# A fifth late expert: its weights loaded and split within the block loop, the experts in natural order, three turns written out

## What is computed

```python
x = _layernorm(x + attention(x, w_qkv, w_out))
probs = softmax(x @ gate_w.T)                     # 16 experts
_, idx = top_k(probs + gate_b, 6)                 # cw: probs of the chosen, else 0
for W1, B1, W2, B2, W3, B3, c in experts:         # 16 of them, H = 176
    h = silu(x @ W1.T + B1) * (x @ W3.T + B3)
    y = y + c[:, None] * (h @ W2.T + B2)
z = silu(x @ ws1.T + bs1) * (x @ ws3.T + bs3) @ ws2.T + bs2     # HS = 352
x = _layernorm(x + y + z)
```

## Time and profile before

| what | us |
| --- | --- |
| median of 3 runs | 1139.32 |
| the runs | 1139.49, 1139.32, 1127.47 |
| the profiled execution, its time | 1130.5 |
| its span, first to last instruction | 1128.7 |

### The profile page before, as it was taken

How to read it: one execution, slowest core, us unless ns; L and a number is a source line. 1 busy time by engine, 2 the same in 40 slices (tenths; PEclk the granted TensorE clock), 3 DMA queues, 4 the chain that set the end, 5 groups by cost and what they waited for, 6 DMA issues and landing times.

```text
span 1128.7 us, 28318 instructions
## 1 busy us (share of the span) xinstructions
PE 1036.1 (92%) x8028; PEld 847.3 (75%) x8029; DVE 748.7 (66%) x2401; ACT 670.9 (59%) x1680; POOL 740.6 (66%) x676
## 2 busy tenths in 40 slices
PE   7899998989898998788998999999999999999991
PEld 4546464646464644387988999999999999999991
DVE  8786878786878787577765555555555555555455
ACT  3567676767676765665555555555555555555544
POOL 4224368787878888877635666666666666666665
PEclk9999999999999998899998999999999999999996
DMA  6624254545454535557867666677776666667593
GB/s 185 183 71 114 77 143 147 164 147 163 148 161 145 169 124 172 189 174 228 287 165 139 115 120 119 114 118 117 119 118 113 110 116 113 116 116 140 82 313 144
DMA packets 127037, 163.54 MB, mean 145 GB/s; under 512 B 18800, under 2 KB 107504, under 8 KB 126704
## 3 DMA queue, kind: packets, MB, share of 16 engines
q1 hardware_dynamic: 82240, 99.73, 31.6%
q0 software_dynamic: 39024, 54.29, 25.6%
q10 hardware_dynamic: 5696, 8.55, 2.4%
HBM read 65.36 MB, written 73.85 MB: 123 GB/s over the span
## 4 chain that ended last, share of the span: by engine, by line
PE 63%; DMA 12%; DVE 12%; issue 5%; ACT 4%; POOL 2%; SPq 1%; ACTq 0%; POOLq 0%; DVEq 0%
PE psum L1057 13%; PE psum L794 10%; PE psum L1084 10%; DMA z_d<-y_sb,tokens 9%; PE psum L836 5%; PE psum L824 4%; PE psum L809 4%; DVE rowmax L1496 3%; PE psum L1042 3%; PE psum L1068 3%; PE psum L1053 3%; PE psum L1023 2%; ACT probs L1160 2%; DMA stack_q<-shift_l 2%; PE psum L811 2%
## 5 line engine op out<-in xcount | busy, mean ns | idle before, releaser
L1160 ACT ACTIVATE probs<-psum 128x512 f32<-128x512 f32 (+2 forms) x384 | 186.5, 530 | 115.1 <-PE psum L824 113.2
L1496 DVE TENSOR_REDUCE rowmax<-psum 128x1 f32<-128x512 f32 (+3 forms) x352 | 211.7, 632 | 60.5 <-PE psum L811 58.7
L2029 POOL DMA_INDIRECT xs_d<-x1p,index x192 | 206.1, 1074 | 53.2 <-issue 40.3
L2103 POOL DMA_INDIRECT x_d<-y_sb,tokens x104 | 162.5, 1562 | 93.6 <-ACT y_sb L1354 65.7
L2103 POOL DMA_INDIRECT z_d<-y_sb,tokens x103 | 160.7, 1560 | 93.7 <-ACT y_sb L1354 51.1
L1835 DVE TENSOR_TENSOR xb_lo<-psum,xb_hi 128x256 fp32r<-128x256 f32 x207 | 87.7, 424 | 201.3 <-ACT xb_hi L1151 199.4
L1057 PE MATMUL psum<-we_hi_lo,xb_hi 128*128 x828 | 200.9, 324 | 0.0
L1354 ACT ACTIVATE y_sb<-psum,combine 128x256 f32<-128x256 f32 x207 | 98.3, 475 | 152.2 <-PE psum L1084 75.2
L1084 PE MATMUL psum<-we_hi_lo,hb_hi 88*128 (+1 forms) x828 | 175.2, 304 | 0.0
L809 PE MATMUL psum<-stack_k,stack_q 96*128 96x256 bf16 (+3 forms) x512 | 139.0, 311 | 9.2 <-DVE rowmax L1496 3.6
L1057 PEld LDWEIGHTS psum<-we_hi_lo,xb_hi 128*128 128x128 f32 x828 | 146.8, 190 | 0.0
(11 more groups left out here) (209 smaller groups left out, 2322.3 us busy)
## 6 DMA issues: line engine op xcount, KB each, us to landing
xb<-xs_d SPq DMA_DIRECT2D x207, 138.0 KB
stack_q<-q_h SPq DMA_DIRECT2D x48, 128.0 KB
stack_k<-k_h SPq DMA_DIRECT2D x45, 128.0 KB
w_raw<-in_we SPq DMA_DIRECT2D x9, 608.0 KB, 4.2
xT_raw<-in_xT SPq DMA_DIRECT2D x9, 512.0 KB, 4.2
stack_q<-q_m SPq DMA_DIRECT2D x32, 128.0 KB
stack_k<-k_m SPq DMA_DIRECT2D x32, 128.0 KB
x_res<-in_x SPq DMA_DIRECT2D x8, 512.0 KB, 3.7
```

The source lines that it names most:

```text
L1160: nc.scalar.activation(probs[kt][:, heads[0]:heads[0] + n, :], st[f % ST_BANKS][:, 0:n * width].rearrange("p (h t) -> p h t", h=n), ACT.Ex ...
L1496: nc.vector.reduce_max(rowmax[gpar][:, heads[0]:heads[0] + n, qt], src, AX.X).then_inc(sm_free, 1)
L2029: nc.gpsimd.indirect_dma_start(out=xs_d[:, :], out_offset=bass.IndirectOffsetOnAxis(ap=index[tp][:, n:n + 1], axis=0), in_=x1p[tp][:, n // ...
L2103: nc.gpsimd.indirect_dma_start(out=(x1_d, z_d)[k % 2][:, :], out_offset=bass.IndirectOffsetOnAxis(ap=tokens[:, k:k + 1], axis=0), in_=y_sb ...
```

## The change

Expert 14 loses its early place. `W_ORDER` becomes 0 to 15 in order, `FIRST_W_AT` loses the step (2, 6), so that items 0 to 4 are split in the last attention batch, and items 5 to 13 (experts 2 to 10, as before) in the shared tiles. The late experts are 11 to 15, five of them. Three turns (24 blocks) are written out instead of two. The last split of the fourth late expert moves from block 15 to 16, its load from behind block 15's rows to behind block 16's; the fifth is loaded behind block 20's and split at 19 and 20 (the places on SyncE are some blocks ahead of the same numbers on the other engines). The calls of `load_w` in the last attention batch, for items 0 to 7, stay as they are.

```diff
-FIRST_W_AT = {(0, 4): 0, (1, 0): 1, (1, 4): 2, (2, 0): 3, (2, 6): 4, (3, 2): 5}
+FIRST_W_AT = {(0, 4): 0, (1, 0): 1, (1, 4): 2, (2, 0): 3, (3, 2): 4}
...
-W_ORDER = (0, 1, 14, 2, 3, 4, 5, 6, 7, 8, 9, 10, 11, 12, 13, 15)
-W_ITEM_AT = {2: 6, 4: 7, 6: 8, 9: 9, 12: 10, 15: 11, 18: 12, 21: 13, 24: 14}
-W_LOAD_AT = {15: 12, 18: 13, 21: 14}
+W_ORDER = tuple(range(E))
+W_ITEM_AT = {2: 5, 4: 6, 6: 7, 9: 8, 12: 9, 15: 10, 18: 11, 21: 12, 24: 13}
+W_LOAD_AT = {15: 11, 18: 12, 21: 13}
...
-LATE_TURNS = 2
-LATE_W_AT = {3: ((0, 0),), 4: ((0, 1),), 7: ((1, 0),), 8: ((1, 1),), 11: ((2, 0),), 12: ((2, 1),), 15: ((3, 0), (3, 1))}
-LATE_LOAD_AT = {5: 0, 8: 1, 12: 2, 15: 3}
+LATE_TURNS = 3
+LATE_W_AT = {3: ((0, 0),), 4: ((0, 1),), 7: ((1, 0),), 8: ((1, 1),), 11: ((2, 0),), 12: ((2, 1),), 15: ((3, 0),), 16: ((3, 1),),
+             19: ((4, 0),), 20: ((4, 1),)}
+LATE_LOAD_AT = {5: 0, 8: 1, 12: 2, 16: 3, 20: 4}
```

## The result

| us | median | runs |
| --- | --- | --- |
| before | 1134.62 | 1139.49, 1139.32, 1127.47, 1129.92 |
| after | 1150.95 | 1153.92, 1154.93, 1145.4, 1147.99 |

The ratio is 1.0146, with a 95% interval of 1.0105 to 1.0186: slower by 1.5%, some 16 us. The forecast was +6.0. The profiled execution of after took 1153.92 us, so the two profiles lie further apart (23.5 us of span) than the two medians. The time lies within the range forecast (up to 1153); a slowdown of over 1%, which came, had been given a chance of 0.22.

A forecast was written before the change was run, and what follows sets the result against it. TensorE, busy 1036.1 of 1128.7 us, was taken as the bound wherever it does not wait. Terms 9.5 + 1.2 - 6.7 + 1.2 + 0.5 + 0.3 = +6.0 on 1139.32 gave 1145.3 us; range 1133.5 (lower edge 1131) to 1153.

The forecast's parts named there:

- The last batch, 0: Last attention batch: the split removed at step (2, 6) lies under a transfer, so nothing gained; at most 1.45 us.
- SyncE's queue, +9.5: Shared tiles: batch 6's stores stand behind load_w(7)'s later wait, holding ScalarE at tile 2 for 9.5 us (6.4 to 11.2).
- The whole chain is late: Shared tiles: everything following ScalarE's hold at tile 2 is late by 9.5 us; later waits move with it, absorbing nothing.
- rival D: Shared tiles: shorter hold of 7.4 us, stores landing 5.8 us after the load's issue; +3.9, 1143.2 us; chance 0.1.
- The clock, +1.2: Shared tiles: after TensorE's 9.9 us idle the lower clock costs 1.2 us (0 to 3.0), some falling into slack.
- Rival C: Shared tiles: the hold costs nothing, as POOL's scatters end the stage; only blocks count, -4.7, 1134.6 us; chance 0.1.
- The blocks, -6.7: Blocks 14 to 16: TensorE's stall goes because block 16's rows no longer wait behind the fourth late load; 6.7 us gained.
- What takes its place, +1.2 +0.5 +0.3: Blocks from 16: rows behind loads at 16 and 20 +1.2, written-out turn's border +0.5, loop entry at 24 +0.3.
- Rival B: Rows behind a late load at 16 or 20 stall again, TensorE idle over 3 us; +12.7, 1152.0 us; chance 0.2.
- the sum: Whole kernel: all terms added, +6.0 us, 1145.3; own range +2 to +10, 1141 to 1149 us; chance 0.6.

The follow-up runs named there:

- three turns: Before with three turns written out instead of two, nothing else changed; ratio 1.0075.
- run 2: Before with one more weight load pulled in front of the stores of batch 6, experts, splits and blocks unchanged; ratio 1.0121.
- Run 7: Before, two turns kept, with the fourth late load issued by ScalarE's queue at block 13 so no rows stand behind it; 1180.44 us, single run.
- run 3: Before with three written turns, the fourth late load behind block 16's rows and its last split at block 16, no fifth late expert; ratio 1.0099.
- run 6: After with one TensorE wait more, at the end of the third written turn, for the add of block 19; 1176.39 us, single run.
- run 9: After with batch 6's store put ahead of expert 4's load, and TensorE's pause at the end of the third turn; ratio to before 1.0018.
- run 10: The kernel of run 3 with two short TensorE pauses, at the ends of the second and third turns; ratio to before 0.9997.
- run 8: After with POOL's indirect transfers overwriting instead of adding, the sum over a token's experts left out; 1162.72 us, single run.

## Why the prediction was right in part, step by step

**The last batch, 0.** Right as far as it can be told. The stretch up to the table load was 3.4 us longer in after, but not by the change. The windows of 460 to 470 us, first before, then after:

```profile
460.00:470.00 10.00, 7.06 (x65) 3.68 (x63) 4.08 (x7) 8.19 (x18) 9.13 (x10) 1.00 0.50 164
```

```profile
460.00:470.00 10.00, 7.48 (x39) 3.91 (x37) 0.36 (x1) 4.76 (x11) 8.96 (x11) 0.66 0.38 134
```

The granted clock fell to the lower level earlier, in the middle of the batch's end. That comes and goes from execution to execution. By the clock of the same 7 us (from 6 us behind the issue of `x_res`), the stretch from that issue to the table load took 21.97, 21.88 and 21.82 us at clocks of 0.92 to 1.00 and 26.32, 26.31 and 24.95 at 0.50 to 0.52, all with the split at (2, 6) in place; without it 22.26 and 20.95 at 0.90 and 1.00, and 25.51 to 25.76 at 0.50 and 0.51. So some 4 us go with the clock in kernels of both kinds, and the split is worth at most 1. One kernel, three turns, has 23.29 at 1.00. What decides the clock here wasn't tried.

**SyncE's queue, +9.5.** Right, in place and size. 10.00 us in after (10.53 on the second chip, 10.46 alone). The term was low by the landing, 7.6 us for 7.1: `x1T_d` was issued 2.3 us behind the end of ScalarE's split (491.27 to 493.60) where I had 2.45. "The whole chain is late" held too: run 2 shows it with nothing given back. The Trainium skill's fit ("DMA: Bandwidth & Descriptors", section "Anatomy of one DMA") would, by my estimate in the prediction, have had the three transfers landed 5.8 us after the first issue. The page gives that fit for one transfer of GpSimd's path, and I put it on three of SyncE's. The trace has 8.5 here (from the load's issue, 0.34 us ahead of the end of its group at 493.08, to 493.60 + 7.6) and 8.0 before. The measurement decides: for these three the estimate is too short, and rival D (a hold of 7.4) fell by it. Why isn't shown; transfers of other queues ran beside them.

**The clock, +1.2.** Mis-sized. ScalarE's t0 is 13.0 us later in after (488.25 to 501.26), its x0 15.8 us later (503.13 to 518.95): 2.8 us were lost between them, at the lower clock. I let part of the 1.5 to 3.0 fall into VectorE's slack; next to nothing of it did. Less the 3.4 us by which the stage began later, t0 is 9.6 us later, x0 12.5 and block 0 13.5: 9.6 for the hold (ScalarE's split ended 0.4 earlier), 2.8 for the clock, and 1.0 behind x0 that I can't place.

**Rival C** (the hold is free) fell with that: POOL was not the late one.

**The blocks, -6.7.** This is the step that failed. Right is that the stall went. Of the 6.7 us that went with it, 2.1 were back by block 16 (4.58 us forecast from block 14 to 16, 6.68 measured). Its mistake was to book the stall as a plain loss, "So the loss goes", and to look for what takes its place only in SyncE's rows. POOL's adds were 15 to 17 us behind at block 14 in both kernels, and the stall was the time in which they caught up. It was a debt that TensorE had to pay, at block 14 in 6.7 us at once, or behind block 16 turn by turn: +2.4 +1.7 +6.9 = +11.0, so that the blocks as a whole are 5.1 us longer where I had them 4.7 shorter. Run 7 (one execution) takes only the stall away and makes the loss, run 3 does it with a third turn beside, runs 6, 9 and 10 show that a stop put elsewhere takes it away, and run 8 that without late adds there is none.

**What takes its place, +1.2 +0.5 +0.3.** Too small and wrong in kind. The two long intervals in blocks 14 to 24 are 4.39 us (15 to 16) and 3.67 us (19 to 20), 2.1 and 1.4 over the usual 2.29, where the border and the two loads had 1.7 together. TensorE waits for no `xb` there. It waits 1.93 and 1.22 us for VectorE's low rows (`xb_lo`), and those for ScalarE, whose copies stood behind a full ring:

```profile
622.69 0.47 ACT L1355 ACTIVATE y_sb<-psum,combine 128x256 f32<-128x256 f32 x1 [3.29 <-DMA x_d<-y_sb,tokens]
...
633.56 0.47 ACT L1355 ACTIVATE y_sb<-psum,combine 128x256 f32<-128x256 f32 x1 [2.57 <-DMA x_d<-y_sb,tokens]
...
624.14 0.42 PE L1054 MATMUL psum<-we_hi_lo,select 98*128 x1 [1.93 <-DVE xb_lo L1836]
```

**Rival B** came near the time (1152.0) by another road. It had the rows behind a late load stall once more, with TensorE idle over 3 us; no such wait exists. That its price was about that of the real mechanism is chance, and it is by this rival, not by the sum, that the range reached up to 1153. The sum's own range for the time, 1141 to 1149, missed; that the miss of the median was 5.7 us and not 10.3 is luck too, the lower median of before. Its phrase on POOL's adds that "grow over these blocks" was as near as the prediction came, and it was put on the landing of rows, not on the adds' own lateness.

**In the numbers.** By the profiles: 3.4 (clock of the attention batch, not the change) + 13.5 + 5.1 (blocks) + 1.5 (tail) = 23.5. Forecast for the change: 10.7 and -4.7. The stages before the blocks account for 2.8 of the miss, the blocks for 9.8. The medians, 16.3 us apart, hold a smaller share of such 3 to 4 us as the clock gives and takes.

**What could have been read from before's trace.** Its own chain of waits: from 700 us on ScalarE's copies already waited 61.8 us for adds, which was on no path that I followed, because I read waits only inside the two stages that the diff touches.

## What to carry to other kernels

Before a stall is booked as a gain, ask who works through it: measure how far each consumer is behind (start of its work for block k less start of the block) on both sides of the stall. If that distance falls there, the stall pays a debt, and without it the debt comes back as waits on the last free buffer, spread thin over the loop, where no single row stands out. And where items of a hand-written queue are renumbered, write out for each call that stays in place what it now waits for, and what stands behind it.

## What the runs showed that I had not expected

- The same loop has two speeds, 18.4 to 18.7 us a turn of eight blocks at lags of 8.5 to 10.9, and 18.8 to 19.1 at 12.7 to 13.2; a lag of 11 to 12 (three turns) drifted up to 13. By the copies' own times the ring of four is full from 12.4. In the slower loop the adds' own pace is 2.36 us a block (after) against 2.32 (before), though ScalarE's copies are some 5.5 us ahead of them there; their landings are longer there: 3.94 us on the mean of blocks 40 to 103 in after, 3.80 and 3.82 in the kernels of runs 10 and 9. Why stays open. A longer ring would test it, and was not run.
- In every kernel but the one with plain writes the lag rises by 0.5 to 1.9 us between blocks 108 and 116 (by 0.3 there). Where it was below 11 it goes on rising, to 2.3 to 3.1 above the old value at 124, and stays up: 10.7 to 13.1 in before, 8.5 to 10.9 with the pause. From there on before itself loops at the slower pace (2.39 us a block). With plain writes it is 8.5 at both ends. What happens there stays open; the kernels without the change show it too.
- The lag is made in the first blocks (10.5 at block 4 of before, 15.2 at 14). After's adds landed in 3.7/4.9/7.0 us (least, median, most) from 592 to 622 us and in 3.6/3.9/4.2 from 700 to 760. The late loads run beside the first of these and not beside the second, but so do other transfers, and no run took the late loads away.
- Transfers that add instead of write cost POOL 1.56 us an issue instead of 0.96, and each table's adds go one behind the other. The Trainium skill ("DMA: Bandwidth & Descriptors", section "Rules for kernel authors") says that such a transfer reads its destination and writes it later with nothing to hold the bytes in between, which is a reason for that order; no run here shows it.
